# Residual sums in eight GpSimd pieces, output products by halves of the queries, and unread products in the layer-0 attention

## The reference

```python
xn = layernorm(x);  x = x + L0_attn(xn) + L0_ffn(xn)
xn = layernorm(x);  x = x + L1_attn(xn) + L1_ffn(xn)
```

```python
for it in range(3):
    ql, kl, vl = qcur[:, :, :16] @ Wlq.T + blq, kcur[:, :, :16] @ Wlk.T + blk, vcur[:, :, :16] @ Wlv.T + blv
    ai = softmax(ln(ql) * tscale @ ln(kl).T / 4) @ vl        # the first 16 positions alone
    diff = mean(abs(iter_out - prev)); attn_out = where(done, attn_out, iter_out)
    done |= (diff < thr + fac * diff) & (it > 0)
    qcur, kcur, vcur = qcur + iter_out, kl, vl
```

```python
att = softmax(where(causal, q @ k.T / 4 + bias, -inf));  y = att @ v;  out = y @ o_w + o_b
```

## Time and profile before

| | us |
|---|---|
| median of 3 runs (lowest, highest) | 2775.09 (2772.73, 2786.11) |
| the profiled execution | 2771.08 |
| its span, from first to last instruction | 2769.0 |
| TensorE busy, share of the span | 94% |
| VectorE, ScalarE, GpSimd busy | 85%, 75%, 50% |
| the parts: prepare, project, attend | 167, 718, 1884 |

### The profile page before, as it was taken

How to read it: one execution, slowest core, us unless ns; L and a number is a source line. 1 busy time by engine, 2 the same in 40 slices (tenths; PEclk the granted TensorE clock), 3 DMA queues, 4 the chain that set the end, 5 groups by cost and what they waited for, 6 DMA issues and landing times.

```text
span 2769.0 us, 57252 instructions
## 1 busy us (share of the span) xinstructions
PE 2605.1 (94%) x21508; PEld 1594.4 (58%) x21508; DVE 2341.9 (85%) x4175; ACT 2073.0 (75%) x3887; POOL 1373.4 (50%) x1768
## 2 busy tenths in 40 slices
PE   4559999999997999999999999999999999999998
PEld 3349989999996445545445454554544545455453
DVE  3358888888886999999989899999998999989894
ACT  2248777887785688788877888878887788887786
POOL 2225555655552355454654545545465454554544
PEclk7579999999999899999999999999999999999999
DMA  2005475554556646465464654646546466464640
GB/s 72 1 31 166 162 191 178 182 181 162 177 173 172 115 71 122 65 112 111 67 115 62 117 103 73 122 62 115 106 71 120 65 113 110 68 118 72 103 86 17
DMA packets 315172, 299.58 MB, mean 108 GB/s; under 512 B 97174, under 2 KB 265516, under 8 KB 314668
## 3 DMA queue, kind: packets, MB, share of 16 engines
q1 hardware_dynamic: 313344, 295.55, 50.0%
q10 hardware_dynamic: 1552, 0.36, 0.1%
HBM read 175.27 MB, written 120.06 MB: 107 GB/s over the span
## 4 chain that ended last, share of the span: by engine, by line
PE 53%; ACT 5%; DMA 4%; issue 1%; DVE 0%; POOLq 0%; POOL 0%; ACTq 0%
PE t_y L1554 18%; PE t_r L1540 15%; PE t_a L1490 12%; ACT t_prob L1584 4%; PE t_a L1524 3%; PE t_r L1501 3%; DMA scr_m<-t_mrows 3%; DMA t_q<-scr_m 1%; ACT t_near L1593 1%; PE t_a L1510 0%; ACT t_mrows L1601 0%; POOLq L1310 0%; POOL t_prob L1727 0%; DVE t_mxd L1639 0%; DVE t_o L1678 0%
## 5 line engine op out<-in xcount | busy, mean ns | idle before, releaser
L1584 ACT ACTIVATE t_prob<-t_r 128x512 f32<-128x512 f32 (+1 forms) x2432 | 1255.7, 596 | 305.8 <-PE t_r L1540 300.5
L1632 DVE TENSOR_REDUCE t_mxc<-t_a 128x1 f32<-128x512 f32 (+3 forms) x1920 | 1130.2, 641 | 95.0 <-PE t_a L1490 86.7
L1540 PE MATMUL t_r<-t_q,t_k 109*128 109x128 bf16 (+4 forms) x4608 | 838.5, 275 | 25.5 <-DMA t_q<-scr_m 14.5
L1490 PE MATMUL t_a<-t_k,t_q 99*128 99x512 bf16 (+3 forms) x2560 | 661.7, 320 | 2.6 <-DVE t_mxc L1632 1.9
L1554 PE MATMUL t_y<-t_prob,t_v 128*32 128x512 f32 (+3 forms) x6144 | 626.5, 497 | 0.0
L1540 PEld LDWEIGHTS t_r<-t_q,t_k 102*128 102x128 bf16 (+1 forms) x4608 | 378.6, 98 | 321.3 <-ACT t_prob L1584 127.4
L1733 POOL TENSOR_SCALAR_AFFINE_SELECT t_near<-t_near 128x512 f32<-128x512 f32 x512 | 332.7, 655 | 449.0 <-ACT t_near L1593 449.0
L1727 POOL TENSOR_SCALAR_AFFINE_SELECT t_prob<-t_prob 128x512 f32<-128x512 f32 x512 | 322.1, 638 | 383.1 <-ACT t_prob L1584 382.3
L1490 PEld LDWEIGHTS t_a<-t_k,t_q 99*128 99x128 bf16 x2560 | 211.8, 99 | 293.3 <-DVE t_mxc L1632 208.2
L1593 ACT COPY t_near<-t_r 128x512 f32<-128x512 f32 x512 | 308.8, 605 | 66.3 <-PE t_r L1501 49.7
L1639 DVE TENSOR_REDUCE t_mxd<-t_near 128x8 f32<-128x1024 f32 x256 | 309.1, 1209 | 45.6 <-POOL t_near L1733 43.9
(11 more groups left out here) (197 smaller groups left out, 4092.4 us busy)
## 6 DMA issues: line engine op xcount, KB each, us to landing
t_q<-scr_q SPq DMA_DIRECT2D x384, 128.0 KB, 4.1
t_k<-scr_k SPq DMA_DIRECT2D x384, 128.0 KB, 6.6
scr_q<-j_part SPq DMA_DIRECT2D x96, 256.0 KB, 3.4
scr_k<-j_part SPq DMA_DIRECT2D x96, 256.0 KB, 2.6
scr_v<-j_v SPq DMA_DIRECT2D x32, 544.0 KB, 5.0
t_v<-scr_v SPq DMA_DIRECT2D x64, 272.0 KB, 8.2
p_x<-in_x SPq DMA_DIRECT2D x32, 512.0 KB, 4.3
scr_res<-j_x SPq DMA_DIRECT2D x32, 512.0 KB, 3.8
```

Source lines behind the costliest of these rows:

```text
L1490: mm = pe.matmul(abank[n % A_BANKS][:, x * w:(x + 1) * w], q_op[t % NG][0:KA, h0 + x, i * P:(i + 1) * P], k_op[t % NG][0:KA, h0 + x, k0:k0 ...
L1540: mm = pe.matmul(ring[n % RING_BANKS][:, s * w + lo:s * w + hi], k_op[g][0:deep, h0 + s, j * P:(j + 1) * P], q_op[g][0:deep, h0 + s, q0 + ...
L1584: nc.scalar.activation(prob[:, q % SLOTS, h0:h0 + m, 0:w], ring[n % RING_BANKS][:, 0:m * w].rearrange("p (h n) -> p h n", h=m), ACT.Exp).t ...
L1632: V.tensor_reduce(mxc[:, t % 2, k0 // 512, h0:h0 + m, i], abank[n % A_BANKS][:, 0:m * w].rearrange("p (h n) -> p h n", h=m), AX.X, ALU.max ...
```

## The change

1. In `prepare`, a helper `fill(n)` puts n products of 256 columns (`ones` by `wqkv`, both there by then) into bank 7, which nobody reads. It is called with 6 before the first deviation of the key, and in each round with 6 before `deviation(0)`, 5 after it, 3 after the first `turn_back`, 8 before the second `products`, and 3 after the second `turn_back`. TensorE waits once more at the start, for constants that GpSimd sets.
2. In `attend`, each quarter of the residual sum is two entries of GpSimd's plan in place of one: eight per batch, each of cost 1300, ready 3000 ns apart, and with a lower priority (rank t + 1.2 and up, before t + 0.6 and up).
3. An output product waits only for the low parts of its own half of the queries; the ranks of the four in the plan go from t + 1.45, 1.57, 1.69, 1.81 to t + 1.0, 1.12, 1.49, 1.61 (a group is 1.0).
4. TensorE's wait for VectorE's first padding (`s_set`) moves from the start of `attend` to the first weighting.

```diff
@@ prepare, TensorE
+            def fill(n):
+                for _ in range(n):
+                    pe.matmul(bank[7][:, 0:D], ones[:, :], wqkv[:, 0, 0, :], start=True, stop=True)
+
             pe.wait_ge(s_in, n_in)
+            pe.wait_ge(s_const, 4)
...
             variance(1, 0)
+            fill(6)
             deviation(1, 0)
             for it in range(ROUNDS):
...
                     variance(1, it + 1)
+                fill(6)
                 deviation(0, it)
+                fill(5)
                 pe.wait_ge(s_nrm[1], it + 1)
...
                 turn_back(2 * it + 1).then_inc(s_sc_pe, 1)
+                fill(3)
                 if more:
                     deviation(1, it + 1)
+                fill(8)
                 for half in range(2):
                     pe.wait_ge(s_pbd[half], it + 1)
...
                 turn_back(2 * it + 2).then_inc(s_pv_pe, 1)
+                fill(3)
@@ plan
-            streams["out"] += [(t + 1.45 + 0.12 * h, "out", t // NG, h) for h in range(OUTS)]
+            streams["out"] += [(t + (1.0 if 2 * h < OUTS else 1.25) + 0.12 * h, "out", t // NG, h) for h in range(OUTS)]
...
             for x in range(OUTS):
-                pl.give("POOL", end + 8000, t + 0.6 + 0.25 * x, ("shift", t // NG, x), 2600)
+                for z in range(2):
+                    pl.give("POOL", end + 8000 + 3000 * (2 * x + z), t + 1.2 + 0.25 * x, ("shift", t // NG, 2 * x + z), 1300)
...
-            ready = max(ready, max(pl.when("ylow", NG * t + n, c) for n in (1, 3) for c in range(2)))
-            ready = max(ready, pl.when("shift", t, x))
+            ready = max(ready, max(pl.when("ylow", NG * t + n, 2 * x // OUTS) for n in (1, 3)))
+            ready = max(ready, pl.when("shift", t, 2 * x + 1))
@@ attend
+        shifts = {(t, x): n + 1 for n, (t, x) in enumerate(e[1:] for e in ORDER["POOL"] if e[0] == "shift")}
...
-                for c in range(2):
-                    for t in (NG * b + 1, NG * b + 3):
-                        pe.wait_ge(s_yl, y_lows[t, c])
+                for t in (NG * b + 1, NG * b + 3):
+                    pe.wait_ge(s_yl, y_lows[t, 2 * x // OUTS])
...
+                if t == 0 and r == 0:
+                    pe.wait_ge(s_set, 1)
...
-            pe.wait_ge(s_set, 1)
...
-                dve.wait_ge(s_shift, 2 * (OUTS * b + x + 1))
+                dve.wait_ge(s_shift, shifts[b, 2 * x + 1])
...
-            def shift(b, x):
-                n = 2 * (OUTS * b + x)
+            def shift(b, n):
+                x, z = divmod(n, 2)
                 mine = res[:, 2 * x:2 * x + 2, :]
...
+                if z == 0:
+                    pool.wait_ge(s_res, 32 * (b + 1))
...
+                    other = obias[:, :].rearrange("p (o n) -> p o n", o=1).to_broadcast([P, 2, D])
+                else:
+                    pool.wait_ge(s_shift, shifts[b, 2 * x])
+                    other = o[:, 2 * x:2 * x + 2, :]
+                pool.tensor_tensor(mine, mine, other, ALU.add).then_inc(s_shift, 1)
```

More of the change, by code:

```diff
@@ L1711, in _ @@
             zero, never = pool.to_reg(0.0), pool.to_reg(BIG)
-            def shift(b, x):
-                n = 2 * (OUTS * b + x)
+            def shift(b, n):
+                x, z = divmod(n, 2)
                 mine = res[:, 2 * x:2 * x + 2, :]
-                pool.wait_ge(s_res, 32 * (b + 1))
-                if b == 0 and x == 0:
-                    pool.wait_ge(s_owin, 16 * N_OW)
-                pool.tensor_tensor(mine, mine, obias[:, :].rearrange("p (o n) -> p o n", o=1).to_broadcast([P, 2, D]),
-                                   ALU.add).then_inc(s_shift, 1)
-                pool.wait_ge(s_shift, n + 1)
-                pool.tensor_tensor(mine, mine, o[:, 2 * x:2 * x + 2, :], ALU.add).then_inc(s_shift, 1)
+                if z == 0:
+                    pool.wait_ge(s_res, 32 * (b + 1))
+                    if b == 0 and x == 0:
+                        pool.wait_ge(s_owin, 16 * N_OW)
+                    other = obias[:, :].rearrange("p (o n) -> p o n", o=1).to_broadcast([P, 2, D])
[3 more added lines that the diff above has]
+                pool.tensor_tensor(mine, mine, other, ALU.add).then_inc(s_shift, 1)
             def mask(t, r):
```

## The result

| | before | after |
|---|---|---|
| median, 4 runs each (lowest, highest), us | 2779.70 (2772.73, 2786.11) | 2739.74 (2730.43, 2741.25) |
| ratio, 95% interval | | 0.985 (0.9813 to 0.9886) |
| the profiled execution, its span | 2771.08, 2769.0 | 2740.79, 2738.7 |

The change made the kernel 1.5% faster. The medians differ by 40 us, the two profiled executions by 30.3; what follows takes the latter apart.

The account below looks back on a forecast made before the run. TensorE was taken as the bound: chained steps largely at half clock in the layer-0 attention, 98.4% busy in the layer-1 middle. Fillers 14, end 4 and middle 1 made 19 us off 2775.1, giving 2756 us, range 2742 to 2776.

Parts of the forecast that it names:

- Fillers: Layer-0 attention: 81 unread products raise TensorE's clock and save 14 us, bounds 0 and 20.
- The overshoot: Layer-0 attention: fillers run at half clock after the variances and don't fit their gaps, costing 1.0 us in each round.
- Rival D: Layer-0 attention: fillers don't hold the clock, win nothing and cost up to 14.5 us; 2771 to 2785 us, chance 0.08.
- Part 2: Layer-1 attention: residual sums in eight spaced pieces change a batch by 0 us, bounds -0.5 to +0.4.
- the prediction's own sign: Layer-1 attention: the forecast is wrong if a batch's length moves by over 0.5 us.
- its main case: Whole kernel: 2756 us, own range 2747 to 2765, the middle within 0.5 us per batch; chance 0.50.
- The middle: Layer-1 attention's 16 batches: output products by halves gain 1 us in total, bounds -12 and +20.
- Rival C: Layer-1 middle: output products spread over two places remove waits, 1 us a batch, 16 us, giving 2740; chance 0.16.
- Rival B: Layer-1 attention: the 1 MB store delays the row maxima's trip, 1.5 us a batch, 24 us, giving 2780; chance 0.14.
- the cover of 8.3 us: Row maxima's trip through memory: 8.3 us from issuing the write until TensorE runs out of work; 3.3 needed undisturbed.
- The tail: End of the kernel: 24 of the last 48 output matmuls move into the last group, saving 4 us, bounds 0 and 5.
- The moved wait: TensorE's wait for VectorE's padding in the layer-1 attention: at most 0.6 us to gain, none taken.

Follow-up runs that it names:

- the fillers alone: Kernel before with only the changed kernel's unread products in `prepare`, attention of before: 2758.3 us, ratio 0.9956.
- the narrow fillers: Kernel before with only the unread products added at the same places, each 8 columns wide instead of 256: 2779.9 us, ratio 1.0024.
- attention alone: Kernel before with items 2 to 4 of the change, without the unread products in `prepare`: 2749.8 us, ratio 0.9917.
- output alone: Kernel before with only item 3, output products waiting by halves and their new ranks: 2767.4 us, ratio 0.9975.
- the later load: Kernel after with the residual's two loads issued behind the trip of the third group's row maxima, sums following: 2711.8 us, ratio 0.9773.

## Why the prediction was wrong

**Fillers (14 us forecast).** Right: 15.6 in the profile, 12 by the times of the fillers alone. `products` takes 1.95 us (forecast 2.2), the turn-back 1.09. The overshoot came where it was expected, behind the variances: there six fillers took 5.47 us in the first round (clock 0.50), 4.29 in the second (0.64) and 4.97 in the third, where they still fitted. Rival D is refuted: the granted clock is 0.88, and 0.86 with the fillers alone. That the gain comes through the clock is what the narrow fillers show.

**Part 2 (0, bounds -0.5 to +0.4 a batch).** This step failed. The spaced sums are worth 1.84 us a batch alone and 1.8 beside the new output order, over three times the bound and some 25 us in 14 batches. I asked what GpSimd's queue would do to the masks and found nothing; for the queue alone that was right (114.19 either way). But the sums' cost, time and rank feed the planner, which wrote another order for the other engines, and that was left out. By the prediction's own sign, a batch's length moving by over 0.5 us, its main case had failed: the mean batch went from 115.36 to 114.26. The change of a cost in a planner is a change of every order that it writes, and the bound was drawn from one engine.

**The middle (1 us).** The bound under it was wrong as well: 98.4% busy was read as little that waits could give back, 26.5 us of 1680, though busy time shrank with the batch itself. The weight loads of the same trace stand 127.4 us for ScalarE, in 327 waits of at most 0.8 us, a sign that was not read. The row of the waits of before, then of after:

```profile
PEld t_r L1540 <- ACT t_prob L1584: 127.4, 327, 0.8
```

```profile
PEld t_r L1553 <- ACT t_prob L1598: 112.2, 265, 0.8
```

The Trainium skill, "Perfetto Trace Analysis", section "Identifying the Most-Contended Engine", calls the matmul's busy share no good measure of how close one is to the roofline. This trace agrees: the same work is 113.5 us busy in the batch shown of before and 111.7 in that of after. Rival C, waits that go for 16 us in the middle, has the size right: its 2740 is what was measured. That is luck. I held its mechanism (output products spread over two places) for the cause, and they gave 0.38 us of floor, not 1; the sums gave the rest, and the scatter and the lead-in moved the sum besides.

**Rival B.** Its collision is there: the store is issued 0.8 us ahead of the maxima's write, which takes 4.6 us in place of 1.5 to 2. It costs nothing that is seen, as the first group's 29.5 to 29.9 us show; the cover of 8.3 us was enough. The median over all writes went from 1.5 to 2.7.

**The scatter.** The second group takes 1.1 us above its shortest before, 2.0 after, and TensorE waits 21.4 us for the maxima after against 14.5. By what the runs show that need not be the change's doing: attention alone has the same orders and 1.0; the kernels range from 0.9 to 2.3, each from one profiled execution.

**The tail (4 us).** 3.1 in the profiled execution, 3.7 in output alone and in attention alone. What is left of the output there, last row of the chain of the kernel after (for the earlier trace rows):

```profile
2727.97 5.18 PE t_a L1537 x24
```

Half the matmuls take 5.18 us, not half of 8.17: the granted clock was 0.55 in this stretch, 0.69 in that of the 48 before. TensorE had waited 4.4 us for the last low part ahead of them.

**The lead-in (nothing forecast, +5.0).** Of it 1.5 is the first batch's last group, which now holds output work. 3.3 lie in the first group, 66.3 us before and 69.6 after; the other kernels stand between 67.0 and 68.8 whatever they change, so most of it may be how the first loads fell out, which was not tested. **The moved wait** brings the first matmul of `attend` 9.2 to 9.3 us behind `project`'s last in place of 9.9 to 10.0, 0.6 to 0.8 sooner where 0.6 was the bound, and nothing of it is seen at the end of the first group.

## What to carry to other kernels

Where a planner writes the order, price a change of its costs or due times as a new order for all engines, not as a move on one: compare the lengths of repeated units, not the waits of the engine that was edited. On a TensorE that looks 98% busy, read the waits of the weight loads as a sign and the distances between starts for the size; the matmul rows of this kernel showed 2.3 us where the weight loads showed 127. And before tuning the order, look at the one unit whose length varies from batch to batch: here the step that took a small transfer from behind a large one gave 1.2%, over half of it by that transfer, and the whole change of the attention 0.8%.

## What was not expected of the hardware

- A 24 KB write to memory lands in 1.4 us at best; in the kernel after it took up to 8.7, and it is slow in two places, behind the residual's 2 MB and behind the store of 1 MB (medians 7.9 and 4.7 us to landing).
- The first step of the join on VectorE, which stood 0.88 us beside a sum on GpSimd, has a median of 193 ns after (before 288) and still reaches 812; with the later load it stays at 377 or less. All those of over 0.6 us stand beside a sum of GpSimd, nearly all beside a mask too. What they cost was not measured.
